# Grouped-query attention phase: maxima subtracted on GpSimd, wide exponentials and all copies on ScalarE, row sums on VectorE

## What is computed

```python
q = hidden_state @ Wq + bq
k = encoder_hidden_state @ Wk + bk
v = encoder_hidden_state @ Wv + bv
scores = jnp.einsum('bkgld,bksd->bkgls', q, k) * scale
scores = scores + encoder_attention_mask[:, :, None, :, :]
attn = jax.nn.softmax(scores, axis=-1)
out = jnp.einsum('bkgls,bksd->bkgld', attn, v)
out = out.transpose(0, 3, 1, 2, 4).reshape(b, l, H)
out = out @ Wo + bo
x = out + hidden_state
return (x - mu) * jax.lax.rsqrt(var + EPS) * gamma + beta
```

## Time and profile before

| | us |
|---|---|
| median of 3 runs | 3429.91 |
| lowest and highest | 3426.48, 3431.15 |
| profiled execution | 3420.91 |
| its span, first to last instruction | 3419.1 |
| group phase in it, first masked scores to last store | about 1201 to 1569 |

### The profile page before, as it was taken

The page is one execution under the profiler, slowest core; times in us unless marked ns, Lnnn a source line. Parts: engine busy times, 40 slices in busy tenths (PEclk is TensorE's granted clock), DMA queues, the critical chain, the costliest instruction groups (busy, mean ns, idle before and its releaser), DMA issues. The chain is left out here.

```text
span 3419.1 us, 52506 instructions
## 1 busy us (share of the span) xinstructions
PE 3161.4 (92%) x19136; PEld 2069.2 (61%) x19136; DVE 1740.4 (51%) x2514; ACT 1162.0 (34%) x4099; POOL 823.1 (24%) x613
## 2 busy tenths in 40 slices
PE   7999899989999988886899999997799999899999
PEld 5666566656666555554676677664455555567675
DVE  4655455520000078885899999997344644400000
ACT  2444234331111166662333444342233433311110
POOL 2333133320000012222555555554000000100000
PEclk9999999989999999999999999998999999999999
DMA  4110131110000141111111111110231110100000
GB/s 161 49 43 30 58 146 58 43 62 25 12 25 12 39 152 52 52 33 66 45 39 43 45 50 44 41 38 29 74 125 34 38 32 24 47 22 34 21 34 13
DMA packets 104307, 170.17 MB, mean 50 GB/s; under 512 B 16512, under 2 KB 54016, under 8 KB 100736
## 3 DMA queue, kind: packets, MB, share of 16 engines
q1 hardware_dynamic: 99296, 124.58, 11.4%
q10 hardware_dynamic: 4896, 44.04, 3.2%
HBM read 135.03 MB, written 33.55 MB: 49 GB/s over the span
## 5 line engine op out<-in xcount | busy, mean ns | idle before, releaser
L2396 POOL TENSOR_TENSOR rec_S<-rec_S,rec_r_t 128x1024 f32<-128x1024 f32 x128 | 302.3, 2362 | 351.6 <-DVE rec_S L2714 350.8
L2714 DVE TENSOR_TENSOR_SCAN rec_S<-rec_decay,rec_S 128x1024 f32<-128x1024 f32 x128 | 299.1, 2336 | 8.9 <-DVE rec_S L2699 4.2
L2076 PE MATMUL mlp_bank<-mlp_src_t,region_a 128*128 128x256 f32 x1024 | 225.3, 383 | 4.1 <-ACT mlp_src_t L1997 4.1
L2076 PE MATMUL pmlp_bank<-pmlp_src_t,region_a 128*128 128x256 f32 x1024 | 224.7, 382 | 1.8 <-ACT pmlp_src_t L1997 1.8
L2088 PE MATMUL mlp_bank<-region_a,mlp_h_t 128*128 128x512 f32 x512 | 221.1, 592 | 0.0
L2088 PE MATMUL pmlp_bank<-region_a,pmlp_h_t 128*128 128x512 f32 x512 | 221.1, 592 | 0.0
L2076 PEld LDWEIGHTS mlp_bank<-mlp_src_t,region_a 128*128 128x128 f32 x1024 | 196.6, 192 | 34.5 <-issue 7.7
L2076 PEld LDWEIGHTS pmlp_bank<-pmlp_src_t,region_a 128*128 128x128 f32 x1024 | 196.1, 192 | 32.2 <-issue 5.5
L1505 ACT ACTIVATE group_scores<-group_scores,group_negmax 128x128 f32<-128x128 f32 x512 | 197.5, 391 | 29.0 <-DVE group_negmax L1599 19.3
L2043 DVE TENSOR_TENSOR mlp_y<-mlp_bank,mlp_xres 128x512 f32<-128x512 f32 x16 | 11.1, 692 | 376.3 <-PE mlp_bank L2088 376.3
L2043 DVE TENSOR_TENSOR pmlp_y<-pmlp_bank,pmlp_xres 128x512 f32<-128x512 f32 x16 | 11.1, 691 | 364.5 <-PE pmlp_bank L2088 364.5
(11 more groups left out here) (370 smaller groups left out, 6509.7 us busy)
## 6 DMA issues: line engine op xcount, KB each, us to landing
rec_vb<-v_by_head SPq DMA_DIRECT2D x32, 512.0 KB, 4.2
region_a<-in_C_w ACTq DMA_DIRECT2D x2, 4096.0 KB, 19.1
region_a<-in_G_w ACTq DMA_DIRECT2D x2, 4096.0 KB, 18.6
self_xres<-in_x SPq DMA_DIRECT2D x16, 256.0 KB, 2.6
rows_A<-self_xres SPq DMA_DIRECT2D x16, 256.0 KB, 2.0
cross_ctx_t<-in_ctx_t SPq DMA_DIRECT2D x16, 256.0 KB, 3.4
cross_xres<-rows_A SPq DMA_DIRECT2D x16, 256.0 KB, 2.7
rows_B<-cross_xres SPq DMA_DIRECT2D x16, 256.0 KB, 2.0
```

The lines of the kernel that those rows point to most:

```text
L2076: product = nc.tensor.matmul(ph.bank(item)[:, i * TT:(i + 1) * TT], W1[:, c, f:f + 128], src_t[:, c, :, :], start=c == 0, stop=c == C - 1)
L2396: nc.gpsimd.tensor_tensor(S[u % 4][:, :, :], S[u % 4][:, :, :], bcast(r_t[:, s.k, UNITS[u][0], :], [128, JH, T], 1), ALU.mult)\
L2714: nc.vector.tensor_tensor_scan(St[:, :, :].rearrange(flat), decay[m][:, :, :].rearrange(flat), St[:, :, :].rearrange(flat), 0.0, ALU.mult, ...
```

## The change

The maxima are no longer a bias of the exponential. GpSimd adds the negated maxima to eight heads at once, in place, with the maxima broadcast along the keys (`subtract_max`, one 128x1024 operation per part, eight per pass), and reports on a new semaphore `shifted`. ScalarE then takes one exponential of 128x1024 per part, without bias and without a second output, and makes all 16 copies of transposed probabilities of a pass, in between. VectorE, which makes none of these copies any more, adds up the rows of each part instead (`row_sum`, eight per pass) and reports on `sum_done`, for which `invert_sums` waits. TensorE's order stays; a transpose now waits for the exponential of its part, that is of eight heads. A part holds the blocks `r` = 0 and 1, or 2 and 3.

```diff
@@ -1297,9 +1297,10 @@
         return [4 * r + b for r in range(4)]
-    def sum_column(u, j):
-        return (2 * (u % 2) + j // 8) * 8 + 2 * (j % 4) + j // 4 % 2
+    def half(tile, part):
+        by_four = tile.rearrange("p (r h) t -> p r h t" if len(tile.shape) == 3 else "p (r h) -> p r h", r=4)
+        return by_four[:, :, 2 * part:2 * part + 2]
     with ExitStack() as stack:
         def sb(name, shape, dt=F32):
@@ -1361,7 +1362,9 @@
         scores_ready = sem("scores_ready")
         scores_read = sem("scores_read")
         max_done = sem("max_done")
+        shifted = sem("shifted")
         exp_done = sem("exp_done")
+        sum_done = sem("sum_done")
         rinv_done = sem("rinv_done")
         rinv_spread = sem("rinv_spread")
         normed = sem("normed")
@@ -1460,19 +1463,36 @@
                                         by_head, bcast(const["ones"][:, 0:NH], [128, NH, HD], 2), ALU.mult)\
                     .then_inc(rinv_spread, 1)
+            def subtract_max(it, u):
+                for part in range(PARTS):
+                    pool.wait_ge(max_done, (it * U + u) * PARTS + part + 1)
+                    numbers = half(S[:, u, :, :], part)
+                    nc.gpsimd.tensor_tensor(numbers, numbers,
+                                            half(negmax[:, u, :], part).unsqueeze(3).to_broadcast([128, 4, 2, T]),
+                                            ALU.add).then_inc(shifted, 1)
             def body(it):
+                later = has_later(it, 1)
+                subtract_max(it, 2)
                 if not is_first(it):
                     scale_output(it - 1, 0)
                 spread_inverse(it, 0)
+                subtract_max(it, 3)
                 residual_bias(it, 0)
                 if not is_first(it):
                     norm_scale(it - 1, 1)
+                if later:
+                    subtract_max(it + 1, 0)
                 spread_inverse(it, 1)
                 if not is_first(it):
                     scale_output(it - 1, 1)
+                if later:
+                    subtract_max(it + 1, 1)
                 residual_bias(it, 1)
                 norm_scale(it, 0)
+            subtract_max(0, 0)
+            subtract_max(0, 1)
             run_ahead(pool, body)
             scale_output(NIT - 1, 0)
             first.scale(pool, following, minus_half)
@@ -1497,14 +1517,9 @@
                 last.then_inc(pj.free_sem(("q", n)), 1)
             def exponentials(it, u, part):
-                if part == 0 and u % UPS == 0:
-                    wait_count(act, rinv_spread, it * 2 + u // UPS - 1)
-                act.wait_ge(max_done, (it * U + u) * PARTS + part + 1)
-                for j in range(part * HP, part * HP + HP):
-                    at = 4 * (j % 4) + j // 4
-                    nc.scalar.activation(S[:, u, at, :], S[:, u, at, :], ACT.Exp, bias=negmax[:, u, at:at + 1],
-                                         accum_out=rowsum[:, u // UPS, sum_column(u, j):sum_column(u, j) + 1])\
-                        .then_inc(exp_done, 1)
+                act.wait_ge(shifted, (it * U + u) * PARTS + part + 1)
+                numbers = half(S[:, u, :, :], part)
+                nc.scalar.activation(numbers, numbers, ACT.Exp).then_inc(exp_done, 1)
             def copy_probs(it, u, r):
                 item = ("t", u, r)
@@ -1514,26 +1529,41 @@
             def body(it):
                 later = has_later(it, 1)
+                copy_probs(it, 0, 0)
                 exponentials(it, 1, 0)
+                copy_probs(it, 0, 1)
                 exponentials(it, 1, 1)
+                copy_probs(it, 0, 2)
                 copy_probs(it, 0, 3)
                 if later:
                     query_features(it + 1, 0)
+                copy_probs(it, 1, 0)
+                copy_probs(it, 1, 1)
                 exponentials(it, 2, 0)
+                copy_probs(it, 1, 2)
                 exponentials(it, 2, 1)
                 copy_probs(it, 1, 3)
                 if later:
                     query_features(it + 1, 1)
+                copy_probs(it, 2, 0)
                 exponentials(it, 3, 0)
+                copy_probs(it, 2, 1)
                 exponentials(it, 3, 1)
+                copy_probs(it, 2, 2)
                 copy_probs(it, 2, 3)
+                copy_probs(it, 3, 0)
+                copy_probs(it, 3, 1)
                 if later:
                     exponentials(it + 1, 0, 0)
                 if has_later(it, 2):
                     rows_features(it + 2)
+                copy_probs(it, 3, 2)
+                copy_probs(it, 3, 3)
                 if later:
                     exponentials(it + 1, 0, 1)
-                copy_probs(it, 3, 3)
                 if is_first(it) and next_weights:
                     next_weights.start(act)
@@ -1600,14 +1630,16 @@
                                         in_=S[:, u, :, :].rearrange("p (r h) t -> p r h t", r=4)[:, :, heads, :],
                                         op=ALU.max, axis=AX.X, negate=True).then_inc(max_done, 1)
-            def copy_probs(it, u, r):
-                item = ("t", u, r)
-                dve.wait_ge(pj.full_sem(item), pj.uses_with(it, item))
-                nc.vector.tensor_copy(PT[:, r, :, :], pj.bank(item)[:, :].rearrange("p (i t) -> p i t", i=4))\
-                    .then_inc(pj.free_sem(item), 1)
+            def row_sum(it, u, part):
+                k, chunk = u // UPS, 2 * (u % UPS) + part
+                if u % UPS == 0 and part == 0:
+                    wait_count(dve, rinv_spread, it * 2 + k - 1)
+                dve.wait_ge(exp_done, (it * U + u) * PARTS + part + 1)
+                nc.vector.tensor_reduce(out=rowsum[:, k, chunk * 8:chunk * 8 + 8].rearrange("p (r h) -> p r h", h=2),
+                                        in_=half(S[:, u, :, :], part), op=ALU.add, axis=AX.X).then_inc(sum_done, 1)
             def invert_sums(it, k):
-                dve.wait_ge(exp_done, it * U * HU + (k + 1) * UPS * HU)
+                dve.wait_ge(sum_done, (it * U + (k + 1) * UPS) * PARTS)
                 nc.vector.reciprocal(rinv[:, k, :], rowsum[:, k, :]).then_inc(rinv_done, 1)
             def copy_inverse(it, k):
@@ -1629,57 +1661,50 @@
             def body(it):
                 later = has_later(it, 1)
-                copy_probs(it, 0, 0)
                 if is_first(it):
                     dve.wait_ge(v_bias_loaded, 16)
                 else:
                     normalise(it - 1, 1)
                 values(it, 0)
-                copy_probs(it, 0, 1)
                 values(it, 1)
-                copy_probs(it, 0, 2)
+                row_sum(it, 0, 0)
                 scale_and_mask(it, 2)
                 row_max(it, 2, 0)
                 row_max(it, 2, 1)
+                row_sum(it, 0, 1)
                 if not is_first(it):
                     output_norm(it - 1, 0)
-                copy_probs(it, 1, 0)
+                row_sum(it, 1, 0)
+                row_sum(it, 1, 1)
                 invert_sums(it, 0)
-                copy_probs(it, 1, 1)
-                copy_probs(it, 1, 2)
                 scale_and_mask(it, 3)
                 row_max(it, 3, 0)
                 row_max(it, 3, 1)
                 copy_inverse(it, 0)
-                copy_probs(it, 2, 0)
                 normalise(it, 0)
                 if later:
                     key_blocks(it + 1, 0)
-                copy_probs(it, 2, 1)
-                if later:
                     key_blocks(it + 1, 1)
-                copy_probs(it, 2, 2)
+                row_sum(it, 2, 0)
                 if later:
                     scale_and_mask(it + 1, 0)
                     row_max(it + 1, 0, 0)
-                if later:
                     row_max(it + 1, 0, 1)
+                row_sum(it, 2, 1)
                 if not is_first(it):
                     output(it - 1, 1)
                     output_stats(it - 1, 1)
-                copy_probs(it, 3, 0)
+                row_sum(it, 3, 0)
+                row_sum(it, 3, 1)
                 invert_sums(it, 1)
-                copy_probs(it, 3, 1)
                 if not is_first(it):
                     output_norm(it - 1, 1)
                 if later:
                     scale_and_mask(it + 1, 1)
                     row_max(it + 1, 1, 0)
-                copy_probs(it, 3, 2)
-                if later:
                     row_max(it + 1, 1, 1)
                 output(it, 0)
                 output_stats(it, 0)
@@ -1776,7 +1801,7 @@
             def transpose_probs(it, u, r):
                 item = ("t", u, r)
                 begin(it, item)
-                pe.wait_ge(exp_done, it * U * HU + u * HU + 4 * (r + 1))
+                pe.wait_ge(exp_done, (it * U + u) * PARTS + r // 2 + 1)
                 for i, slot in enumerate(slots(r)):
                     last = nc.tensor.transpose(pj.bank(item)[:, i * 128:i * 128 + 128], S[:, u, slot, :], ident)
                 last.then_inc(pj.full_sem(item), 1)
```

## The result

| | before | after |
|---|---|---|
| median of 5 runs (us) | 3426.48 | 3444.47 |
| lowest and highest | 3422.06, 3431.15 | 3441.79, 3449.37 |
| profiled execution, its span | 3420.91, 3419.1 | 3448.80, 3446.7 |

The changed kernel is slower: the ratio is 1.0057, 95% interval 1.0044 to 1.0069, some 18 us. The time lies within the range of the prediction and 13 us above its forecast of 3431. That forecast started from a median of 3429.91 and added 1.5; against the median of 3426.48, 18 us came. It said "no change", so it was off by more than a measurement can tell.

A forecast was written before the change was run, and what follows sets the result against it. TensorE, busy 39.81 of a 44.51 us pass, was taken as the bound; 1.8 + 2.8 - 1.2 + 6 x 0.0 - 1.9 = +1.5 us on a median of 3429.91 gave about 3431 us, range 3417 to 3452.

The forecast's parts named there:

- rival 1: VectorE's normalisation is held through both GpSimd subtractions, likewise beside those of unit 2: 20 us, 3451 us; chance 0.14.
- rival 2: Subtraction, hand-off or exponential each 0.5 us longer, delaying value projection v1 by 0.5 to 1.6 us a pass: 3439; chance 0.13.
- the normalisation's end: On VectorE beside GpSimd: starts at 1381.56, ends 0.27 us after the first subtraction, at 1382.43.
- The subtraction: On GpSimd, 128x1024, eight a pass: priced at 2.36 us each like the bias addition, 18.9 us in all.
- Leg 1: VectorE from the masked scores to value projection v1, 18.34 us: to grow by 0.39 us.
- Leg 2: TensorE from value projection v1 to the next masked scores, 26.17 us: to fall by 0.39 us.
- The four-engine queue: ScalarE's copy of transposed rows stands behind exponential, subtraction and VectorE's statistics: new TensorE wait of 1.08 us at unit 3's third transpose.
- The output wait: TensorE's output projection waits for VectorE's output, now behind a row sum: from 1.23 to 2.36 us.
- Rival 3: TensorE's waits close as ScalarE gains slack: half of 4.70 us in six passes, 14 us, 3417; chance 0.16.
- Head: Start of the phase: first transposes wait for subtraction and exponential instead of four small exponentials, +1.8 us once.
- Weight loads: After pass 0, ScalarE's copies follow the load issues: first weighing waits 6.7 us, not 3.9, +2.8; other transition waits go, -1.2.
- The last pass: TensorE's 1.85 us wait for VectorE's inverse sums, no longer queued behind its copies, goes: -1.9 us.

The follow-up runs named there:

- experiments 1 and 2: Changed kernel with the normalisation as scalar_tensor_tensor: 3450.08 us; with row sum (it,2,1) moved behind the output: 3440.39 us; with both edits: 3447.30 us.
- experiment 3: Changed kernel with each GpSimd subtraction of 128x1024 done as two of 128x512: 3436.21 us.
- experiment 7: Kernel before with all copies of probabilities on ScalarE and nothing else of the change: 3424.39 us; with the weight loads also in two blocks: 3418.23 us.

## Why the prediction was right in its range and wrong in its mechanism, step by step

The range of 3417 to 3452 holds the result only because it was stretched to take in rival 1, at a chance of 0.14; rival 2 alone reached to 3439. The sum itself, a pass of 44.5 us and 3426 to 3436, missed.

- **The step that failed** in the sum is the normalisation's end, "I let it end 0.27 after the first subtraction". The rule was right in the kernel before, the change, the kernel with the sum behind the output and the one with the copies alone: it ends 0.27 to 0.28 us after a GpSimd instruction. What that instruction is was wrong. The sum had the normalisation start 1.76 us into a subtraction of 2.36; measured, it starts 2.01 us into the pair and the first takes 1.90, so it misses the first's end by 0.1 us and is held through the second. Price per normalisation: 2.03 us, against 0.87.
- **The other normalisation** was in no term of the forecast, only in rival 1. It takes 1.96 us for 0.54. Made 0.26 us longer, it lengthens the pass by as much (experiments 1 and 2); of 0.70 us less, 0.38 came back (experiment 3).
- **Rival 1** was the mechanism, with 3.3 us a pass on top and a hold through both subtractions. It is through the second alone, and 1.75 us net. It had 0.14; its condition, that the normalisation meets the second subtraction, hung on two tenths of a microsecond, and such a condition deserves even odds.
- **The subtraction** was priced by the row it shares a shape with, 2.36, whose second operand repeats along an outer axis, and not by twice the row with a broadcast operand, 2.1. The second was nearer, and by it (first end 1381.9, start 1381.56) the hold would still have come out at the first. A cheaper GpSimd operation made the result worse. The exponential took 1.063 us, the 1.06 of its row; the estimate of 1.13 was for a form with a pointer bias, which this one no longer has.
- **Leg 1** was to grow by 0.39 us and grew by 1.77. **Leg 2** was to give back 0.39 and gave nothing: TensorE's wait at the key block is 0.77 instead of 0.4, behind the held first normalisation.
- **The four-engine queue** was overrated, in the sum and more so in rival 2: a wait of 0.38 instead of 1.08 us, as the subtraction was cheaper. The output wait, 2.36, was right to 0.01. **Rival 3** didn't happen in the change, but the copies alone show its mechanism: 1.28 us a pass.
- **Once-only terms.** Head: +1.8 foreseen, +1.9 measured. Weight loads: 10.2 us of ScalarE, near the 9.7 foreseen, but TensorE's wait is 4.58, not 6.7; with a first held normalisation in it the stretch costs 2.2, where the sum had 2.8 - 1.2. The last pass was to gain 1.9 and lost 4.2. It had VectorE's wait go and did not ask who is late next: the inverse sums now stand behind two maxima, three row sums and the held normalisation, and TensorE has nothing else to do.

The rows of that place, of the changed kernel, TensorE's wait first and then windows of 3 us (columns as in the earlier trace rows; the clock is the third number from the right):

```profile
1555.27 1.08 PE L1830 MATMUL group_pjP<-ident,group_rinv_by_feature 128*128 128x128 f32 x4 [4.02 <-POOL group_rinv_by_feature L1462]
```

```profile
1552.00:1555.00 3.00, 0.00 (x0) 0.00 (x0) 2.96 (x4) 0.63 (x2) 2.89 (x3) 0.83 0.36 97
1555.00:1558.00 3.00, 2.72 (x16) 1.63 (x16) 2.96 (x3) 0.00 (x0) 0.65 (x2) 0.50 0.20 78
1558.00:1561.00 3.00, 1.83 (x13) 1.11 (x14) 2.96 (x5) 2.12 (x3) 3.00 (x2) 0.50 0.00 0
1561.00:1564.00 3.00, 3.00 (x7) 1.72 (x7) 1.09 (x1) 1.53 (x2) 1.46 (x2) 0.50 0.00 0
1564.00:1567.00 3.00, 3.00 (x18) 1.23 (x16) 0.00 (x0) 0.58 (x1) 0.00 (x0) 0.96 0.00 0
```

After 4 us without work TensorE runs at 1.2 GHz, the lower of its two levels, for some 9 us; the four transposes take 1.08 us and not 0.66. Behind its last masking the kernel before has a granted clock of 0.92 up to the last normalisation, the change 0.75. TensorE is busy there for 22.79 us before and for 25.52 in the change, on no more work by the records (156 matmuls against 136), and idle for 7.15 and 8.65. So both idle time and clock are in the 4.2 us, and the clock has the larger part; how exactly they divide stays open. Taking this wait away is not enough: the copies alone don't have it, and take 33.2 us there, with the other waits of experiment 7. Why the clock is lower in some steady passes and not in others, with the same waits, stays open too.

## What to carry over

When a change gives GpSimd long work, look for VectorE instructions beside it that are a tensor_scalar from SBUF or read two SBUF tensors, and ask which GpSimd instruction will be under way when each starts: that one's whole rest is the price, and the start time has to be known better than the forecast can know it, so carry both cases. Move such instructions to where GpSimd is idle, or cut GpSimd's instructions short. And try the parts of a change one by one: here one part gains 1.3 us a pass and the rest costs 3.

## What the runs showed of the hardware

- A VectorE operation that GpSimd holds goes on when one GpSimd instruction ends, even when the next follows without a gap: 1.33 us beside 128x512 subtractions, 2.03 beside 128x1024 ones, 0.91 when only the tail of one was left, each for an operation of 0.54. The GpSimd instruction that runs when it gets in took 1.23 us for 1.05.
- A scalar_tensor_tensor with both tensors in SBUF is held like the tensor_scalar (2.2 to 2.3 us for 0.75); two reductions (2.35 us) and the masking from PSUM (2.29 us) are not.
- GpSimd adds a 128x1024 tile and an operand that repeats along the innermost axis in 1.90 us, faster than the 2.36 with a 128x128 operand that repeats along the outer axes.
- 13 DMA issues in a row held ScalarE for 10 us; its last three took 1.30, 2.30 and 2.78 us. Split into 7 and 6, no issue took over 0.8 and the blocks held it for 2.8 and 1.4.
- With the 13 weight loads ahead of it in SyncE's list, the context load was issued 15 us later, and TensorE waited 5.25 us for it.
